# Rounding to integers by casts through int32 instead of a magic constant, in the FFN block of a layer-norm, attention and BitLinear layer on 8 cores

## The chip, the cores and the metric

The kernel runs on the 8 cores of one Trainium2 chip, the same program on each, with no exchange between them. The metric is the device time of the slowest core in microseconds (us). The engines of a core are called PE (TensorE, matrix products and transposes), DVE (VectorE), ACT (ScalarE), POOL (GpSimd) and SP (SyncE, which here only issues DMAs).

## The reference

With `xn = layernorm(x)`, the output is `x + attention(xn) + ffn(xn)`. The change concerns the ffn alone:

```
def act_quant(x):
    scale = 127.0 / jnp.clip(jnp.max(jnp.abs(x), axis=-1, keepdims=True), 1e-05)
    q = jnp.clip(jnp.round(x * scale), -128.0, 127.0) / scale
    return x + jax.lax.stop_gradient(q - x)
def bitlinear158(x, w, b):
    xq = act_quant(rms_norm(x))
    wq = weight_quant(w)
    return jnp.einsum('bsd,od->bso', xq, wq) + b
h = jax.nn.silu(bitlinear158(x, w1, b1))
h = jax.nn.gelu(h, approximate=False)
h = layer_norm(h, ln_g, ln_b)
return bitlinear158(h, w2, b2)
```

x is 4 x 4096 x 2048 float32, w1 is 8192 x 2048, w2 is 2048 x 8192. The two places that matter are the two `jnp.round(x * scale)` on activations: one on the 2048 wide input of w1, one on the 8192 wide input of w2.

## The kernel before

Each core owns 2048 rows (16 tiles of 128) of one of the four batches. The program goes through phases with a barrier of all engines between them: quantising w1 and w2 to ternary values in DRAM (phase_q), layer norm and the K, V and Q projections with rope (phase_a, phase_b1, phase_b2, phase_b3), the ffn (phase_f) and the attention (phase_att), which adds the stored ffn result. The change touches phase_f only.

phase_f works on 8 blocks (index fb) of FB = 256 rows. The activations of a block lie transposed, channel on the partition and row in the free dimension, so one piece is 128 x 256; the hidden layer has OC = 64 such pieces, the model width DC = 16. Every engine has one queue, and the order in it is the order of the code. For block fb, with pb = fb - 1, the queues hold in this order:

- mm1: PE forms 64 products with w1 (L1066, 16 matmuls each, weights fST loaded by SP in 32 loads of 1 MB into two buffers). DVE takes each out of one of four PSUM banks (L1085, L1089), ACT takes a tanh (L1104), DVE multiplies (L1094, a scalar_tensor_tensor), and ACT applies the gelu and the sums for the second layer norm.
- The statistics of that layer norm (small operations on DVE, ACT and PE), and then the loop of DVE that normalises the 64 pieces of fH (L1275 to L1290). Beside it PE forms mm2 of the block before, pb (L850, weights fW in 32 loads of 1 MB into two buffers); after every fourth piece DVE takes one of the 16 results out of PSUM into one of two buffers fTF20 and fTF21 (`evac_mm2`, L863), and ACT adds the bias into fFT (L873).
- `emit_a1(fb + 1)`: the input of the next block. For its two 128 x 2048 tiles DVE and ACT do a layer norm (L431 to L438), then DVE scales and rounds each tile in place (L990 and L993), PE transposes it in 16 pieces (L478) and ACT copies these to fXQT (L493). A scale row is spread over the partitions into bcd (L229).
- The Q2 loop: DVE scales and rounds the 64 pieces of fH to the bf16 integers fQ2, the right operand of mm2. This is the loop of L1372 and L1374. Each piece is two instructions, each with a drain behind it, in which DVE waits until its writes are done:

```
vector.tensor_mul(b["TF"][:, :], H[:, oc * FB:(oc + 1) * FB], s.bcc[:, :])
vector.drain()
ins = vector.tensor_scalar(Q2[:, oc * FB:(oc + 1) * FB], b["TF"][:, :],
                           MAGIC, MAGIC, ALU.add, ALU.subtract)
```

- `emit_b_base(pb)`: PE transposes the 32 pieces of fFT of block pb back through two PSUM banks (L914), DVE adds x (fXN, loaded again from x_own) into fBB (L935), and SP stores fBB to base_scr in four parts. Then mm1 of the next block begins. In block 0 there is no pb, so mm1 of block 1 stands on PE right behind `emit_a1(1)`.

After the eighth block mm2 and the base part of that block follow alone. The rounding uses that adding and subtracting 12582912 (MAGIC) in float32 leaves the nearest integer.

Of the kernel before, what the change touches and what calls it, by code (L numbers as in the profile page):

```python
# [8 lines left out]

F32 = mybir.dt.float32  # L10
BF16 = mybir.dt.bfloat16
AF = mybir.ActivationFunctionType
ALU = mybir.AluOpType
AX = mybir.AxisListType

MAGIC = 12582912.0
NEGBIG = -1.0e9


# [20 lines left out]
class Bld:  # L40
# [745 lines left out]
    def phase_f(self, b):  # L786
        s, c, block = self, self.c, self.block
        D, DC, OC, FB, INNER = c.D, c.DC, c.OC, c.FB, c.INNER
        NT = FB // 128
        H, Q2, XQT = b["H"], b["Q2"], b["XQT"]  # L790

        csx, csd, cq1 = "F_sx", "F_sd", "F_q1"
        ctt, cte2 = "F_ct", "F_ce"
# [10 lines left out]
        cm2, cm2e, cffn = "F_m2", "F_m2e", "F_ff"  # L804
# [7 lines left out]
            s.sem(nm)  # L812
        n_ocg = OC // 4
        OH = OC // 2
        XPO = max(1, D // FB)

        def emit_b_w2(pb, fb2):
# [38 lines left out]

        def evac_mm2(vector, pb, fb2, dc):
            vector.wait_ge(s.sem(cm2), fb2[cm2] + 2 * (dc + 1))
            if dc >= 2:
                vector.wait_ge(s.sem(cffn), fb2[cffn] + dc - 1)  # L860
            elif pb > 0:
                vector.wait_ge(s.sem(cffn), fb2[cffn])
            ins = vector.tensor_mul(b["TF2"][dc % 2][:, :], s.PB[2 + dc % 2][:, 0:FB],  # L863
                                    s.bce[:, :])
            s.inc(ins, cm2e, 1)
# [76 lines left out]

        def emit_a1(fbk):
            t0k = fbk * FB
            a1B = {nm: s.val(nm) for nm in (csd, ctt, "F_Ttp", cq1, csx)}
            XNF, cxn, cfree, base = self.emit_ln(s.x_own[t0k:t0k + FB, :], NT, "F_L", b,
                                                 pre=[(csx, a1B[csx]),
                                                      ("F_Ttp", a1B["F_Ttp"])])
            q1base = a1B[cq1]

            @block.scalar
            def _(scalar):
                for t in range(NT):
                    scalar.wait_ge(s.sem(cxn), base[cxn] + t + 1)
                    ins = scalar.activation(b["SQD"][:, :], XNF[t % 2][:, :], AF.Square,
                                            accum_out=s.fst[:, 16 + t:17 + t])
                    s.inc(ins, csx, 1)
                    scalar.drain()
                    ins = scalar.activation(s.fst[:, 18 + t:19 + t], s.fst[:, 16 + t:17 + t],
                                            AF.Sqrt, bias=s.eps_col[:, 0:1], scale=1.0 / D)  # L960
                    s.inc(ins, csd, 1)

            @block.vector
            def _(vector):
                vector.wait_ge(s.sem(ctt), a1B[ctt])
                for t in range(NT):
                    vector.wait_ge(s.sem(csd), a1B[csd] + t + 1)
                    vector.reciprocal(s.fst[:, 0:1], s.fst[:, 18 + t:19 + t])
                    vector.drain()
                    vector.reduce_max(s.fst[:, 1:2], XNF[t % 2][:, :], AX.X,  # L970
                                      apply_absolute_value=True)
                    vector.drain()
                    vector.tensor_mul(s.fst[:, 2:3], s.fst[:, 0:1], s.fst[:, 1:2])
                    vector.drain()
                    vector.tensor_scalar_max(s.fst[:, 2:3], s.fst[:, 2:3], 1e-5)
                    vector.drain()
                    vector.reciprocal(s.fst[:, 3:4], s.fst[:, 2:3])
                    vector.drain()
                    vector.tensor_mul(s.fst[:, 3:4], s.fst[:, 3:4], s.fst[:, 0:1])
                    vector.drain()  # L980
                    vector.tensor_scalar_mul(s.fst[:, 3:4], s.fst[:, 3:4], 127.0)
                    vector.drain()
                    vector.tensor_mul(s.fst[:, 20 + t:21 + t], s.fst[:, 2:3], s.m1h_sb[:, 0:1])
                    vector.drain()
                    vector.tensor_scalar_mul(s.fst[:, 20 + t:21 + t], s.fst[:, 20 + t:21 + t],
                                             1.0 / 127.0)
                    vector.drain()
                    if t == 0:
                        vector.wait_ge(s.sem("F_Ttp"), a1B["F_Ttp"])
                    vector.tensor_scalar(b["Q1"][t % 2][:, :], XNF[t % 2][:, :],  # L990
                                         s.fst[:, 3:4], MAGIC, ALU.mult, ALU.add)
                    vector.drain()
                    ins = vector.tensor_scalar(b["Q1"][t % 2][:, :], b["Q1"][t % 2][:, :],  # L993
                                               MAGIC, None, ALU.subtract)
                    s.inc(ins, cq1, 1)

            self.emit_transpose(b["Q1"], cq1, None, q1base, NT,
                                lambda t, dc: XQT[:, dc * FB + t * 128: dc * FB + t * 128 + 128],
                                "F_T")

            @block.tensor
            def _(tensor):
                tensor.wait_ge(s.sem(cq1), q1base + NT)
                tensor.wait_ge(s.sem("F_Tte"), s.val("F_Tte"))
                ins = None
                for t in range(NT):
                    ins = tensor.transpose(s.PB[6][0:1, t * 128:t * 128 + 128],
                                           s.fst[:, 20 + t:21 + t], s.ident_f[:, :])
                s.inc(ins, ctt, 1)

            @block.scalar
            def _(scalar):
                scalar.wait_ge(s.sem(ctt), s.val(ctt))
                ins = scalar.copy(s.srow[0:1, 0:FB], s.PB[6][0:1, 0:FB])
                s.inc(ins, cte2, 1)

            self.bcast_row(s.srow[0:1, 0:FB], s.bcd[:, :], FB, 7, "F_cs",
                           cte2, s.val(cte2))

        emit_a1(0)  # L1020
        for fb in range(c.NFB):
# [344 lines left out]
            @block.vector  # L1366
            def _(vector):
                vector.wait_ge(s.sem(f3), s.val(f3))
                if pb >= 0:
                    vector.wait_ge(s.sem(cm2), fB[cm2] + 2 * DC)  # L1370
                for oc in range(OC):
                    vector.tensor_mul(b["TF"][:, :], H[:, oc * FB:(oc + 1) * FB], s.bcc[:, :])  # L1372
                    vector.drain()
                    ins = vector.tensor_scalar(Q2[:, oc * FB:(oc + 1) * FB], b["TF"][:, :],  # L1374
                                               MAGIC, MAGIC, ALU.add, ALU.subtract)
                    s.inc(ins, cq2, 1)
                    vector.drain()

# [466 lines left out]
    def build(self):  # L1845
# [3 lines left out]
        D, KV, DC, OC, FB = c.D, c.KV, c.DC, c.OC, c.FB  # L1849
# [7 lines left out]
        with self.ctx:  # L1857
            for i in range(8):
                self.sem(f"bar{i}")
            with nc.Block() as block:  # L1860
# [3 lines left out]
                if self.upto >= 1:  # L1864
                    st = ExitStack()
                    a = alloc(st, [("qW0", [128, 2048], F32), ("qW1", [128, 2048], F32),
                                   ("qS0", [128, 2048], BF16), ("qS1", [128, 2048], BF16),
                                   ("qT0", [128, 2048], BF16), ("qT1", [128, 2048], BF16)])
# [6 lines left out]
                if self.upto >= 2:  # L1875
# [4 lines left out]
                    a = alloc(st, [("aXA", [128, D], F32), ("aXN0", [128, D], F32),  # L1880
                                   ("aXN1", [128, D], F32), ("aSQ", [128, D], BF16)])
# [5 lines left out]
                    if self.upto >= 3:  # L1887
                        st = ExitStack()
                        a = alloc(st, [("kKH", [128, DC * 512], F32),
                                       ("kWC0", [128, D], BF16), ("kWC1", [128, D], BF16),  # L1890
                                       ("kTR0", [128, 1024], F32), ("kTR1", [128, 1024], F32),
                                       ("kKO0", [128, 512], BF16), ("kKO1", [128, 512], BF16),
                                       ("kRT0", [128, 512], F32), ("kRT1", [128, 512], F32)])
# [6 lines left out]
                    if self.upto >= 4:  # L1900
                        st = ExitStack()
                        a = alloc(st, [("vWV", [128, DC * (D // 2)], BF16),
                                       ("vKO0", [128, 512], BF16), ("vKO1", [128, 512], BF16)])
# [22 lines left out]
                if self.upto >= 6:  # L1926
# [10 lines left out]
                                   ("fHS2", [128, FB], BF16), ("fHS3", [128, FB], BF16),  # L1937
                                   ("fTG0", [128, FB], F32), ("fTG1", [128, FB], F32),
                                   ("fTF", [128, FB], F32),
                                   ("fTF20", [128, FB], F32), ("fTF21", [128, FB], F32),  # L1940
                                   ("fRM", [128, FB], F32),
                                   ("fRN", [128, FB], F32),
                                   ("fW20", [128, (OC // 2) * 128], BF16),
# [7 lines left out]
                                 HB=[a["fHB0"], a["fHB1"], a["fHB2"], a["fHB3"]],  # L1951
                                 HS=[a["fHS0"], a["fHS1"], a["fHS2"], a["fHS3"]],
                                 TG=[a["fTG0"], a["fTG1"]],
                                 TF=a["fTF"], TF2=[a["fTF20"], a["fTF21"]],
                                 XNF0=a["fXN0"], XNF1=a["fXN1"],
                                 RM=a["fRM"], RN=a["fRN"],
                                 W2=[a["fW20"], a["fW21"]], FT=a["fFT"],
# [94 lines left out]
```

## Time and profile before

| | |
|---|---|
| median of 2 runs | 10460.79 us (10424.76 and 10496.82) |
| the profiled execution's own time | 10498.86 us |
| its span on the slowest core (core 4) | 10497.3 us |
| spans of the 8 cores | 10396.2 to 10497.3 us |
| busy on that core | PE 4937.4, DVE 3670.3, ACT 2248.3, POOL 230.3 us |
| phase_f | about 4615 to 8800 us of the span |

The span is the time from the first to the last instruction of a core; the 1.6 us between it and the execution's own time lie around it. No engine is busy for half of the span, so busy shares alone do not say what sets the time: the phases differ, and within phase_f the engines mostly work in turn. The views to read are the waits of an engine (who released it), the instructions in order of time, and the busy time by stretches.

### The profile page before, as it was taken

Reading aid. Unit: us, or ns where it says so; the run is one execution under the profiler, and the core shown is the slowest. Engines: PE = TensorE matmul, PEld = TensorE weight load, DVE = VectorE, ACT = ScalarE, POOL = GpSimd, SP = SyncE. Lnnn points to the kernel's source line nnn. Section 1 sums busy time; section 2 is a strip of 40 time slices with the busy share of each in tenths; the row PEclk is TensorE's granted clock in tenths of the full one; section 3 lists DMA queues with packets and bytes.
Section 4 is the critical chain, followed back from the end, with each engine's and each line's share of the span. In section 5 each row is a group of like instructions: output and inputs, shape, how many; then the busy total and the mean of one; then the engine's idle time right before and its main releaser. Section 6 shows DMA issues by size and latency. Waiting matters only on the chain.

```text
span 10497.3 us, 91973 instructions; the slowest of 8 cores (10396.2 to 10497.3 us)
## 1 busy us (share of the span) xinstructions
PE 4937.4 (47%) x27826; PEld 2905.6 (28%) x28008; DVE 3670.3 (35%) x8144; ACT 2248.3 (21%) x4838; POOL 230.3 (2%) x214
## 2 busy tenths in 40 slices
PE   0000002454456853343566564747484854665656
PEld 0000002221122321222344443435363532222222
DVE  5521113112211012226565747475656541111120
ACT  0055444200001111222313131313141300111110
POOL 0000000011110000000000000000000000000000
PEclk9999995666777876676787777878686877787879
DMA  6678982576772145552344343435352535232324
GB/s 233 245 246 230 177 161 85 91 89 97 95 89 59 48 75 90 87 106 83 121 148 153 133 149 133 169 117 181 115 189 104 188 138 148 89 108 85 116 67 134
DMA packets 949922, 1356.91 MB, mean 129 GB/s; under 512 B 564032, under 2 KB 785600, under 8 KB 840896
## 3 DMA queue, kind: packets, MB, share of 16 engines
q1 hardware_dynamic: 546720, 1233.57, 37.5%
q0 software_dynamic: 402720, 117.45, 11.1%
q8 instruction: 236, 3.87, 0.1%
q14 instruction: 246, 2.02, 0.1%
HBM read 1325.70 MB, written 142.61 MB: 140 GB/s over the span
## 4 chain that ended last, share of the span: by engine, by line
DMA 34%; PE 29%; DVE 20%; ACT 6%; issue 6%; DVEq 4%; SPq 1%; ACTq 0%; POOLq 0%
PE PB L1066 7%; DMA qW<-w2t 5%; PE PB L628 5%; PE PB L746 4%; DMA qW<-w1t 4%; DMA kWC<-wk 4%; DMA fST<-w1q_scr 3%; DMA fW<-w2q_scr 3%; PE PB L850 3%; PE PB L1479 3%; DMA tVB<-v_scr 2%; DVE fTF L1372 2%; DMA q3WC<-wq 2%; DMA kt_scr<-kKO 2%; DMA y<-tOB 2%
## 5 line engine op out<-in xcount | busy, mean ns | idle before, releaser
L850 PE MATMUL PB<-fQ,fW 128*128 128x256 bf16 x8192 | 1000.6, 285 | 252.8 <-DMA fW<-w2q_scr 244.7
L1066 PE MATMUL PB<-fXQT,fST 128*128 128x256 bf16 x8192 | 1022.4, 281 | 200.1 <-DMA fST<-w1q_scr 118.4
L850 PEld LDWEIGHTS PB<-fQ,fW 128*128 128x128 bf16 x8192 | 823.7, 102 | 432.4 <-issue 304.8
L1066 PEld LDWEIGHTS PB<-fXQT,fST 128*128 128x128 bf16 x8192 | 784.6, 100 | 424.6 <-issue 320.2
L628 PE MATMUL PB<-xnT,kWC 128*128 128x512 bf16 x2007 | 606.0, 472 | 606.9 <-ACT kKH L641 338.2
L543 PE MATMUL PB<-ident_f,aXN 128*128 128x128 f32 x512 | 114.2, 416 | 1255.5 <-DVE aXN L530 1003.7
L746 PE MATMUL PB<-vWV,xnT 128*128 128x512 bf16 x2007 | 471.9, 398 | 120.0 <-DMA vWV<-wv 117.2
L628 PEld LDWEIGHTS PB<-xnT,kWC 128*128 128x128 bf16 x2048 | 232.9, 116 | 979.8 <-issue 894.3
L543 PEld LDWEIGHTS PB<-ident_f,aXN 128*128 128x128 f32 x512 | 103.9, 224 | 1265.7 <-issue 1265.7
L399 DVE TENSOR_TENSOR qT<-qS 128x2048 bf16<-128x2048 bf16 x128 | 156.9, 1226 | 806.9 <-ACT qS L387 806.9
L692 DVE TENSOR_TENSOR kRT<-kKH,kTR 128x512 f32<-128x512 f32 x64 | 44.3, 692 | 1001.7 <-ACT kKH L641 789.6
L1690 PE MATMUL PB<-tPT,tVB 128*128 128x512 bf16 x1252 | 313.9, 394 | 165.2 <-DMA tVB<-v_scr 136.5
L1479 PE MATMUL PB<-tKB,tQA 128*128 128x512 bf16 x1128 | 295.2, 426 | 193.8 <-DMA tKB<-kt_scr 192.3
L314 DVE TENSOR_REDUCE absacc<-qW 128x1 f32<-128x2048 f32 x128 | 292.6, 2286 | 260.0 <-DMA qW<-w1t 131.3
L1832 DVE TENSOR_TENSOR tOB<-PB,tBP 128x128 f32<-128x128 f32 x256 | 74.7, 292 | 861.7 <-PE PB L1741 603.3
L914 PE MATMUL PB<-ident_f,fFT 128*128 128x128 f32 x256 | 111.9, 443 | 539.4 <-DVE fBB L935 529.4
L386 ACT ACTIVATE qS<-qW,sm 128x2048 bf16<-128x2048 f32 x128 | 256.2, 2001 | 461.3 <-DMA qW<-w2t 314.8
L628 PE MATMUL PB<-q3XQ,q3WC 128*128 128x512 bf16 x1000 | 280.4, 446 | 135.8 <-DMA q3WC<-wq 128.0
L1094 DVE SCALAR_TENSOR_TENSOR fH<-fTG,fTF 128x256 f32<-128x256 f32 x512 | 217.9, 426 | 354.5 <-ACT fTG L1104 354.5
L1085 DVE TENSOR_TENSOR fTF<-PB,bcd 128x256 f32<-128x256 f32 x512 | 217.6, 425 | 291.8 <-PE PB L1066 283.2
L746 PEld LDWEIGHTS PB<-vWV,xnT 128*128 128x128 bf16 x2048 | 207.8, 102 | 384.1 <-issue 216.3
L641 ACT COPY kKH<-PB 128x512 f32<-128x512 f32 x128 | 74.2, 586 | 1120.1 <-PE PB L628 689.6
(230 smaller groups left out, 6696.5 us busy)
## 6 DMA issues: line engine op xcount, KB each, us to landing
fST<-w1q_scr SPq DMA_DIRECT2D x256, 1024.0 KB, 5.0
fW<-w2q_scr SPq DMA_DIRECT2D x256, 1024.0 KB, 5.2
qW<-w1t SPq DMA_DIRECT2D x128, 1024.0 KB, 6.3
qW<-w2t SPq DMA_DIRECT2D x128, 1024.0 KB, 7.7
tVB<-v_scr SPq DMA_DIRECT2D x160, 512.0 KB, 3.3
kWC<-wk POOLq DMA_DIRECT2D x128, 512.0 KB, 7.4
tKB<-kt_scr SPq DMA_DIRECT2D x40, 1024.0 KB, 7.9
w1q_scr<-qT SPq DMA_DIRECT2D x64, 512.0 KB, 3.5
```

The lines of the kernel that those rows point to most:

```text
L314: ins = vector.reduce_sum(s.absacc[:, na % 64:na % 64 + 1], WROWS[it % 2][:, 0:cw], AX.X, apply_absolute_value=True)
L386: scalar.activation(SGN[0][:, 0:cw], WROWS[it % 2][:, 0:cw], AF.Sign, bias=nmh)
L543: ins = tensor.transpose(bank[:, (dc % 4) * 128:(dc % 4) * 128 + 128], src[:, dc * 128:(dc + 1) * 128], s.ident_f[:, :])
L628: ins = tensor.matmul(bank[:, :], WCB[it % 2][:, dci * 128:(dci + 1) * 128], rhs_cb(tb, dci), start=(dci == 0), stop=(dci == DC - 1))
L746: ins = tensor.matmul(bank[:, 0:VW], s.xnT[:, dci * c.KV + kt * 128: dci * c.KV + kt * 128 + 128], wvh[:, dci * (D // 2) + do * VW: dci * ...
L850: ins = tensor.matmul(bank[:, 0:FB], b["W2"][it % 2][:, oo * 128:(oo + 1) * 128], Q2[:, oc * FB:(oc + 1) * FB], start=(oc == 0), stop=(oc ...
L1066: ins = tensor.matmul(bank[:, 0:FB], b["ST"][g % 2][:, dc * 256 + o2 * 128: dc * 256 + o2 * 128 + 128], XQT[:, dc * FB:(dc + 1) * FB], sta ...
L1085: ins = vector.tensor_mul(b["TF"][:, :], s.PB[MBK[oc % 4]][:, 0:FB], s.bcd[:, :])
L1094: ins = vector.scalar_tensor_tensor(H[:, oc * FB:(oc + 1) * FB], b["TG"][oc % 2][:, :], 1.0, b["TF"][:, :], ALU.add, ALU.mult)
L1372: vector.tensor_mul(b["TF"][:, :], H[:, oc * FB:(oc + 1) * FB], s.bcc[:, :])
L1479: last = tensor.matmul(bank[:, :], b["QA"][:, dc * 512 + il * 128: dc * 512 + il * 128 + 128], b["KB"][nktc % 2][:, d8 * 512:(d8 + 1) * 51 ...
L1690: last = tensor.matmul(s.PB[d8][:, :], b["VB"][nvc % 2][:, dc * 128:(dc + 1) * 128], b["PT"][:, kc * 512:(kc + 1) * 512], start=(kc == 0), ...
```

## The change

Both roundings are done another way. The value is shifted up by 256 (RSH) so that it is positive, cast to int32 (new buffer fQI) and back to float32; a comparison adds one where the fraction is at least a half, and 256 is taken off again. In the Q2 loop a piece is now six instructions in place of two, each followed by a drain. In `emit_a1` the second instruction on a 2048 wide tile is replaced by eight pieces of 256 columns with four instructions each. The two buffers fTF20 and fTF21 become one (fTF20), so `evac_mm2` waits for ACT to have read the previous result (`cffn` one step later than before). Before the first tile of `emit_a1` DVE also waits for the stores of fBB that were issued up to then (F_bs0, F_bs1). The two constants I32 and RSH and a local name DH that is not used are added.

```diff
@@ evac_mm2
-            if dc >= 2:
-                vector.wait_ge(s.sem(cffn), fb2[cffn] + dc - 1)
+            if dc >= 1:
+                vector.wait_ge(s.sem(cffn), fb2[cffn] + dc)
@@ emit_a1
-            a1B = {nm: s.val(nm) for nm in (csd, ctt, "F_Ttp", cq1, csx)}
+            a1B = {nm: s.val(nm) for nm in (csd, ctt, "F_Ttp", cq1, csx,
+                                            "F_bs0", "F_bs1")}
@@
                     if t == 0:
                         vector.wait_ge(s.sem("F_Ttp"), a1B["F_Ttp"])
+                        vector.wait_ge(s.sem("F_bs0"), a1B["F_bs0"])
+                        vector.wait_ge(s.sem("F_bs1"), a1B["F_bs1"])
                     vector.tensor_scalar(b["Q1"][t % 2][:, :], XNF[t % 2][:, :],
-                                         s.fst[:, 3:4], MAGIC, ALU.mult, ALU.add)
-                    vector.drain()
-                    ins = vector.tensor_scalar(b["Q1"][t % 2][:, :], b["Q1"][t % 2][:, :],
-                                               MAGIC, None, ALU.subtract)
+                                         s.fst[:, 3:4], RSH, ALU.mult, ALU.add)
+                    vector.drain()
+                    ins = None
+                    for hq in range(D // FB):
+                        q1c = b["Q1"][t % 2][:, hq * FB:(hq + 1) * FB]
+                        vector.tensor_copy(b["QI"][:, :], q1c)
+                        vector.drain()
+                        vector.tensor_copy(b["TF"][:, :], b["QI"][:, :])
+                        vector.drain()
+                        vector.scalar_tensor_tensor(b["RN"][:, :], q1c, -0.5,
+                                                    b["TF"][:, :], ALU.add, ALU.is_ge)
+                        vector.drain()
+                        ins = vector.scalar_tensor_tensor(q1c, b["TF"][:, :], -256.0,
+                                                          b["RN"][:, :], ALU.add, ALU.add)
+                        vector.drain()
                     s.inc(ins, cq1, 1)
@@ the Q2 loop
                     vector.tensor_mul(b["TF"][:, :], H[:, oc * FB:(oc + 1) * FB], s.bcc[:, :])
                     vector.drain()
-                    ins = vector.tensor_scalar(Q2[:, oc * FB:(oc + 1) * FB], b["TF"][:, :],
-                                               MAGIC, MAGIC, ALU.add, ALU.subtract)
+                    vector.tensor_scalar(b["TF"][:, :], b["TF"][:, :], RSH, None, ALU.add)
+                    vector.drain()
+                    vector.tensor_copy(b["QI"][:, :], b["TF"][:, :])
+                    vector.drain()
+                    vector.tensor_copy(b["RM"][:, :], b["QI"][:, :])
+                    vector.drain()
+                    vector.scalar_tensor_tensor(b["RN"][:, :], b["TF"][:, :], -0.5,
+                                                b["RM"][:, :], ALU.add, ALU.is_ge)
+                    vector.drain()
+                    ins = vector.scalar_tensor_tensor(Q2[:, oc * FB:(oc + 1) * FB],
+                                                      b["RM"][:, :], -256.0,
+                                                      b["RN"][:, :], ALU.add, ALU.add)
                     s.inc(ins, cq2, 1)
                     vector.drain()
@@ buffers
-                                   ("fTF20", [128, FB], F32), ("fTF21", [128, FB], F32),
+                                   ("fQI", [128, FB], I32),
+                                   ("fTF20", [128, FB], F32),
-                                 TF=a["fTF"], TF2=[a["fTF20"], a["fTF21"]],
+                                 TF=a["fTF"], QI=a["fQI"], TF2=[a["fTF20"], a["fTF20"]],
```

The first place is DVE's queue from the last instruction of `emit_a1(1)` into the Q2 loop of block 0. Before (fXN is the input tile, fH the hidden layer, fQ the rounded hidden layer, bcc and bcd scale rows spread over the partitions):

```order
L990 TENSOR_SCALAR fXN<-fXN,fst 128x2048
L993 TENSOR_SCALAR fXN<-fXN 128x2048
L226 UNCONDITIONAL_BRANCH
L229 COPY bcd<-PB 128x256
L1366 UNCONDITIONAL_BRANCH
L1372 TENSOR_TENSOR fTF<-fH,bcc 128x256
L1374 TENSOR_SCALAR fQ<-fTF 128x256
```

The same place on DVE in the changed program, from the last 256 wide piece of `emit_a1(1)` through the first piece of the Q2 loop:

```order
L1002 CAST fQI<-fXN 128x256
L1004 CAST fTF<-fQI 128x256
L1006 SCALAR_TENSOR_TENSOR fRN<-fXN,fTF 128x256
L1009 SCALAR_TENSOR_TENSOR fXN<-fTF,fRN 128x256
L228 UNCONDITIONAL_BRANCH
L231 COPY bcd<-PB 128x256
L1383 UNCONDITIONAL_BRANCH
L1389 TENSOR_TENSOR fTF<-fH,bcc 128x256
L1391 TENSOR_SCALAR fTF<-fTF 128x256
L1393 CAST fQI<-fTF 128x256
L1395 CAST fRM<-fQI 128x256
L1397 SCALAR_TENSOR_TENSOR fRN<-fTF,fRM 128x256
L1400 SCALAR_TENSOR_TENSOR fQ<-fRM,fRN 128x256
```

Nothing has changed places with anything else: the new instructions stand where the old one stood, and the copy of bcd and the loop behind it come after them. The six rows from L1389 to L1400 stand 64 times in a row, and the four from L1002 to L1009 eight times in a row for each tile. DVE has 9804 instructions in the changed program and 7260 before: 4 more for each of 512 pieces and 31 more for each of 16 tiles.

## Rows read from the trace of the kernel before

**Rows 1.** The page: span.

```profile
span 10497.3 us, 91973 instructions; the slowest of 8 cores (10396.2 to 10497.3 us)
```

**Rows 2.** Busy by stretch: length, PE, PEld, DVE, ACT, POOL, PE clock, DMA share, GB/s.

```profile
4615.00:8800.00 4185.00, 2413.21 (x18128) 1785.26 (x18128) 2406.26 (x6280) 1063.55 (x2704) 8.50 (x16) 0.78 0.40 142
```

**Rows 3.** Waits of PE in phase_f: total us, times, longest.

```profile
PE PB L914 <- DVE fBB L935: 529.4, 42, 58.1
PE PB L478 <- DVE fXN L993: 325.3, 16, 91.9
```

**Rows 4.** PE in order of time: around two Q2 loops, start us, us.

```profile
5060.48 8.52 PE L1066 MATMUL PB<-fXQT,fST 128*128 128x256 bf16 x64
5118.96 3.57 PE L1066 MATMUL PB<-fXQT,fST 128*128 128x256 bf16 x16 [49.95 <-DVE fTF L1085]
...
5575.74 3.88 PE L914 MATMUL PB<-ident_f,fFT 128*128 128x128 f32 x8 [58.10 <-DVE fBB L935]
...
5613.83 6.38 PE L1066 MATMUL PB<-fXQT,fST 128*128 128x256 bf16 x31 [7.54 <-DMA fST<-w1q_scr]
```

**Rows 5.** DVE in order of time: the Q2 loop of block 0.

```profile
5061.00 0.41 DVE L1372 TENSOR_TENSOR fTF<-fH,bcc 128x256 f32<-128x256 f32 x1
5061.49 0.29 DVE L1374 TENSOR_SCALAR fQ<-fTF 128x256 bf16<-128x256 f32 x1
5061.88 0.43 DVE L1372 TENSOR_TENSOR fTF<-fH,bcc 128x256 f32<-128x256 f32 x1
...
5117.86 0.29 DVE L1374 TENSOR_SCALAR fQ<-fTF 128x256 bf16<-128x256 f32 x1
5118.38 0.42 DVE L1085 TENSOR_TENSOR fTF<-PB,bcd 128x256 f32<-128x256 f32 x1 [0.23 <-issue]
```

**Rows 6.** Groups of DVE by line and shape: busy us, mean ns, idle before.

```profile
L1372 DVE TENSOR_TENSOR fTF<-fH,bcc 128x256 f32<-128x256 f32 x512 | 218.0, 426 | 49.0 <-issue 3.2
L1094 DVE SCALAR_TENSOR_TENSOR fH<-fTG,fTF 128x256 f32<-128x256 f32 x512 | 217.9, 426 | 354.5 <-ACT fTG L1104 354.5
L1374 DVE TENSOR_SCALAR fQ<-fTF 128x256 bf16<-128x256 f32 x512 | 150.4, 294 | 41.6 <-issue 2.6
L1285 DVE COPY fRM<-fH 128x256 f32<-128x256 f32 x8 | 2.4, 294 | 0.7
L229 DVE COPY bcc<-PB 128x256 f32<-128x256 f32 x8 | 3.4, 425 | 36.7 <-PE PB L222 36.7
L692 DVE TENSOR_TENSOR kRT<-kKH,kTR 128x512 f32<-128x512 f32 x64 | 44.3, 692 | 1001.7 <-ACT kKH L641 789.6 <-DMA kt_scr<-kKO 212.1
```

**Rows 7.** DVE in order of time: rounding the two tiles in emit_a1(2).

```profile
5499.23 1.29 DVE L990 TENSOR_SCALAR fXN<-fXN,fst 128x2048 f32<-128x2048 f32 x1
5500.60 1.23 DVE L993 TENSOR_SCALAR fXN<-fXN 128x2048 f32<-128x2048 f32 x1
5501.74 0.16 DVE L968 RECIPROCAL fst<-fst 128x1 f32<-128x1 f32 x1
```

**Rows 8.** PE in order of time: the transposes of the second tile.

```profile
5508.71 3.65 PE L478 MATMUL PB<-ident_f,fXN 128*128 128x128 f32 x16 [3.09 <-DVE fXN L993]
```

**Rows 9.** Busy by stretch: mm1, mm2, the Q2 loop of block 1; columns as rows 2.

```profile
5120.00:5275.00 155.00, 135.45 (x1088) 96.30 (x1086) 77.47 (x198) 94.00 (x260) 0.00 (x0) 0.96 0.58 204
5290.00:5440.00 150.00, 114.18 (x900) 93.01 (x900) 119.91 (x296) 8.76 (x16) 0.00 (x0) 0.90 0.51 190
...
5516.00:5574.90 58.90, 1.64 (x4) 0.58 (x4) 46.36 (x129) 0.00 (x0) 0.00 (x0) 0.50 0.01 4
```

**Rows 10.** The costliest groups of the page: the matmuls of mm2 and mm1.

```profile
L850 PE MATMUL PB<-fQ,fW 128*128 128x256 bf16 x8192 | 1000.6, 285 | 252.8 <-DMA fW<-w2q_scr 244.7
L1066 PE MATMUL PB<-fXQT,fST 128*128 128x256 bf16 x8192 | 1022.4, 281 | 200.1 <-DMA fST<-w1q_scr 118.4
```

**Rows 11.** DVE and ACT in order of time: a result of the last mm2.

```profile
8608.52 0.43 DVE L863 TENSOR_TENSOR fTF<-PB,bce 128x256 f32<-128x256 f32 x1 [9.37 <-PE PB L850]
...
8609.04 0.51 ACT L873 ACTIVATE fFT<-fTF,b2r_sb 128x256 f32<-128x256 f32 x1 [9.29 <-DVE fTF L863]
```

More of the change, by code:

```diff
@@ L10 @@
 F32 = mybir.dt.float32
+I32 = mybir.dt.int32
 BF16 = mybir.dt.bfloat16
@@ L16 @@
 MAGIC = 12582912.0
+RSH = 256.0
 NEGBIG = -1.0e9
@@ L814, in phase_f @@
         OH = OC // 2
+        DH = D // 2
         XPO = max(1, D // FB)
```

## The prediction

> **What bounds the kernel now.** I went from the whole to the place. The page gives a span of 10497.3 us [rows 1], and the busy time by stretches says that phase_f takes 4185 us of it, with PE busy for 2413 and DVE for 2406 of these [rows 2]. Two engines that are each busy for 58% of a stretch and idle for the rest are either both waiting for a third or for each other. So the next view is who waited for whom: in phase_f PE sat for 529.4 us in front of the transposes of the ffn result (L914) until DVE had done an addition, 42 times and once for 58.1 us, and for 325.3 us in front of the transposes of the rounded input (L478) until DVE had rounded it, 16 times [rows 3]. The engines take turns, and in these two places it is DVE's turn.
>
> The order of time shows what DVE does then. Around the Q2 loop of block 1 the next transposes wait for 58.10 us, and around that of block 0 the next products of mm1 wait for 49.95 us, after the 64 matmuls that fit into the four free banks took 8.52 us [rows 4]. In block 0 the loop runs from 5061.00 us to 5118.38 us, which is when the first use of a mm1 result (L1085) starts: 64 pieces in 57.4 us, 0.89 us each, with no wait for another engine between them [rows 5]. In the stretch of block 1's loop PE is busy for 1.64 us, ACT for none and the DMA engines at a share of 0.01 [rows 9]. So the Q2 loop stands alone on the path to the end in each of the 8 blocks, and what is added to it is added to the time. Behind it the 32 additions start, their four stores and the second load of x follow in series, and the loads of mm1 are issued only after that (7.54 us of waiting for fST before mm1 [rows 4]). None of these lies beside the loop, so a longer loop hides none of them.
>
> The rounding in `emit_a1` is in series too. The first tile's L993 ends and the second tile's work follows on DVE at once [rows 7]; the transposes of the second tile wait for the second L993 (3.09 us idle, releaser L993) [rows 8], and the copies, the row bcd and the Q2 loop hang on these.
>
> **The change part by part.** Prices first. At 128x256 a tensor_scalar with constants takes 294 ns, a copy in SBUF 294, a two-operand instruction 426, and a scalar_tensor_tensor on two float32 operands also 426 [rows 6]. Between two instructions with a drain between them about 0.08 us pass: L1372 and L1374 take 426 + 294 = 720 ns and repeat every 0.89 us [rows 5, 6], so 0.17 for two.
>
> Q2 loop, for each piece. Unchanged: the multiplication. Removed: one tensor_scalar of 0.294. Added: one tensor_scalar (0.294 + 0.08 = 0.374), two casts, two scalar_tensor_tensor. For a cast between float32 and int32 there is no row. It is a copy with one source, both sides in SBUF, four bytes in and four out. The nearest row is the copy from SBUF to SBUF, 294 ns; the other end is the copy out of PSUM, 425 ns, which is also what a two-operand instruction takes. L1374 also changes the type (float32 to bf16) and is at 294. I take 0.294 + 0.08 = 0.374 a cast. No row of this width with one or two operands is under 286 to 294 ns, so I see no end below. The scalar_tensor_tensor with the comparison: 0.426 + 0.08 = 0.506. The last one takes the place of the removed instruction: 0.426 - 0.294 = 0.132. Sum: 0.374 + 2 x 0.374 + 0.506 + 0.132 = 1.76 us. With 64 pieces and 8 blocks: 512 x 1.76 = 901 us. A piece then takes 2.65 us and a loop 170 us.
>
> The Trainium skill bears on the cast: VectorE: DVE Perf Modes, section "What auto-detection actually checks", says that an instruction with one source takes two elements a cycle when source and destination are in SBUF, whatever the type. By that rule the casts cost what the SBUF copy does, and the sum stays; without it they cost what the copy from PSUM does.
>
> `emit_a1`, for each tile. Removed: L993, 1.14 us from its start to the next instruction on the first tile and 1.23 us to its end on the second [rows 7], so 1.2. Added: eight times two casts and two scalar_tensor_tensor, each with a drain: 8 x (2 x 0.374 + 2 x 0.506) = 14.1 us. Net 12.9 us, and with 16 tiles 206 us. The first tile's transposes now run beside the second tile's rounding as before; the second tile's wait grows from 3.09 us to about 16.
>
> One buffer for fTF2: in the last mm2 DVE's evacuation starts at 8608.52 us, ACT reads the buffer from 8609.04 for 0.51 us, and DVE had idled 9.37 us before its turn [rows 11]. The new wait is over some 8 us before it matters: nothing. Were the cover gone, it would be 1.03 us for each of 15 results in 8 blocks, 124 us. The waits for the fBB stores name stores issued a block earlier, which were over before DVE came to this point: nothing; without that cover, at most a wait like the 7.54 us for a DMA in rows 4, 8 times, 60 us.
>
> Sum: 901 + 206 = 1107 us. The profiled execution took 10498.86 us, so it would be 11606. Its own time lies 38 us above the median of the runs shown (10460.79 us), and I forecast the median: 11568 us, about 10.6% more.
>
> **The rivals.**
>
> The casts run at one element a cycle. For: no row has int32 in it. Against: a changed type does not slow L1374, and the copies. There are 2 x (512 + 128) = 1280 casts, each 425 - 294 = 131 ns longer: +168 us, 11736 us. The full sum would then be 1275 us.
>
> PE's clock gives something back. The granted clock is 0.96 in mm1, 0.90 in mm2 and 0.50 in the Q2 loop [rows 9]. If longer rests of the array led to the full clock in all of mm1 and mm2, 16384 matmuls of 256 columns would take 107 ns at 2.4 GHz, 1748 us in place of 1000.6 + 1022.4 = 2023 [rows 10]: at most 275 us back, so 11293 us. Against: the array already rests for 58 us in each block and these stretches are near the full level, and mm2 waits for its weights for 244.7 us beside [rows 10], so a faster clock there would largely turn into waiting. The opposite, later starts at the half level, is as small: transposes and mm1's first products behind the loop start at 0.50 already.
>
> The comparison is dear. In the scalar_tensor_tensor, two float32 operands in SBUF might stream at half the rate: 256 columns more, which by the step from 426 ns at 256 columns to 692 at 512 [rows 6] is 266 ns. 1280 such instructions give +340 us, 11908 us. Against it stands L1094, the same instruction on two float32 operands in SBUF, at 426 ns in 512 cases [rows 6]. The Trainium skill, Vector Engine (DVE) Microarchitecture Reference, section "7. Points that are easy to get wrong", says that this instruction form with two SBUF sources other than bf16 has half the throughput; that is this rival if it is read against one element a cycle, and the trace does not agree with that reading.
>
> Not slower. For that the added time must lie under something else that ends later anyway: one mechanism, DVE's two stretches not being what the next stage waits for. The most that lies beside a Q2 loop is mm1's first 8.52 us in block 0 [rows 4], already covered now, and 1.64 us of PE in block 1 [rows 9]. To stay within 2% (209 us) some 900 of the 1107 us would have to be covered, 112 us in each block; fully covered it would be 10461 us. The rows speak against it in every block. That the change does not do what it says could only mean that a drain costs nothing, or that instructions overlap: without the 0.08 us gaps the sum would be about 1107 - (4 x 512 + 32 x 16) x 0.08 = 902 us, 11363 us; the gaps are seen in rows 5, with the same drains.
>
> **How the numbers follow.** The forecast with casts as copies: 0.80. Casts at the lower rate: 0.11. Clock giving back over 60 us, or gaps smaller than counted: 0.05. The dear comparison: 0.03. Not slower: 0.01. Within the forecast's own case, the two runs of before differ by 72 us, and gap and cover add some 40 us either way: 11490 to 11650. The range must reach over the second case, which holds most of the rest: 11460 to 11760 us. A measurement of this kernel can tell about 2% from no change. Faster by over 2%: 0.005. Within 2%: 0.015. Slower: 0.98.
>
> **What would show it.** Right: the casts at 294 ns and the scalar_tensor_tensor at 426; a piece of the Q2 loop every 2.65 us and the loop 170 us; PE's longest wait before L914's transposes near 171 us; 15.5 us in place of 2.6 for rounding a tile; mm1 and mm2 stretches as long as before; the phases outside phase_f unchanged. Wrong: casts near 425 ns (rival one); a scalar_tensor_tensor near 690; an idle DVE inside the Q2 loop or before an evacuation of mm2 that ACT releases (the wait on one buffer); or a Q2 loop whose growth PE or DMA work fills.

## The result, and the profile after

The changed kernel takes 11528.42 us (median of 11 runs, 11456.07 to 11604.1); the kernel before took 10420.11 us beside it (10 runs). The ratio is 1.104, with a 95% interval of 1.1003 to 1.1076: 1108 us more. The forecast was 11568 us, from a sum of 1107 us. Every ratio here is formed from fast executions alone (the cores of one chip half sometimes run some per cent slower together), so it can differ by up to 0.6% from the quotient of the medians given beside it.

Line numbers in the rows of a changed kernel or of an experiment are those of that kernel's own code.

The groups of DVE of the changed kernel, in the columns of [rows 6]:

```profile
L1400 DVE SCALAR_TENSOR_TENSOR fQ<-fRM,fRN 128x256 bf16<-128x256 f32 x512 | 217.9, 426 | 38.5
...
L1397 DVE SCALAR_TENSOR_TENSOR fRN<-fTF,fRM 128x256 f32<-128x256 f32 x512 | 217.5, 425 | 40.4 <-issue 3.1
...
L1391 DVE TENSOR_SCALAR fTF<-fTF 128x256 f32<-128x256 f32 x512 | 150.5, 294 | 39.6 <-issue 0.6
L1393 DVE CAST fQI<-fTF 128x256 int32<-128x256 f32 x512 | 150.5, 294 | 39.7 <-issue 3.1
L1395 DVE CAST fRM<-fQI 128x256 f32<-128x256 int32 x512 | 150.5, 294 | 38.8 <-issue 1.7
```

The casts, for which the trace before had no row, cost 294 ns in both directions, what the copy and the tensor_scalar cost in [rows 6]. The comparison (L1397) costs what the other scalar_tensor_tensor does. The last column gives the idle time ahead of all 512, 0.08 us for each instruction.

DVE in order of time, the first and the last piece of the Q2 loop of block 0, against [rows 5]:

```profile
5011.94 0.41 DVE L1389 TENSOR_TENSOR fTF<-fH,bcc 128x256 f32<-128x256 f32 x1
5012.44 0.29 DVE L1391 TENSOR_SCALAR fTF<-fTF 128x256 f32<-128x256 f32 x1
5012.80 0.29 DVE L1393 CAST fQI<-fTF 128x256 int32<-128x256 f32 x1
5013.17 0.29 DVE L1395 CAST fRM<-fQI 128x256 f32<-128x256 int32 x1
5013.54 0.43 DVE L1397 SCALAR_TENSOR_TENSOR fRN<-fTF,fRM 128x256 f32<-128x256 f32 x1
5014.04 0.43 DVE L1400 SCALAR_TENSOR_TENSOR fQ<-fRM,fRN 128x256 bf16<-128x256 f32 x1
5014.56 0.42 DVE L1389 TENSOR_TENSOR fTF<-fH,bcc 128x256 f32<-128x256 f32 x1
...
5180.12 0.43 DVE L1400 SCALAR_TENSOR_TENSOR fQ<-fRM,fRN 128x256 bf16<-128x256 f32 x1
5180.78 0.42 DVE L1102 TENSOR_TENSOR fTF<-PB,bcd 128x256 f32<-128x256 f32 x1 [0.23 <-issue]
```

From one multiplication to the next a piece takes 2.62 us, and the loop takes 168.8 us, against 0.89 and 57.4 before: 111.4 us more, and 8 x 111.4 = 891 us.

PE around it, which answers to [rows 4] and [rows 8]:

```profile
4983.85 3.65 PE L480 MATMUL PB<-ident_f,fXN 128*128 128x128 f32 x16 [42.39 <-DVE fXN L1009]
5003.40 3.64 PE L480 MATMUL PB<-ident_f,fXN 128*128 128x128 f32 x16 [15.91 <-DVE fXN L1009]
...
5011.43 9.93 PE L1083 MATMUL PB<-fXQT,fST 128*128 128x256 bf16 x64
5181.35 3.38 PE L1083 MATMUL PB<-fXQT,fST 128*128 128x256 bf16 x16 [159.99 <-DVE fTF L1102]
```

PE waits 159.99 us where it waited 49.95. Its wait for the second tile is 15.91 us where it was 3.09 in block 1 [rows 8] and in block 0. Its wait for the first tile is 42.39 us, where the trace before has at the same place:

```profile
5046.13 3.65 PE L478 MATMUL PB<-ident_f,fXN 128*128 128x128 f32 x16 [29.60 <-DVE fXN L993]
5052.87 3.48 PE L478 MATMUL PB<-ident_f,fXN 128*128 128x128 f32 x16 [3.09 <-DVE fXN L993]
```

Each is 12.8 us longer, and 16 x 12.8 = 205 us. The waits of PE in phase_f, against [rows 3]:

```profile
PE PB L917 <- DVE fBB L938: 1296.9, 42, 170.4
```

Again 42 times, and the longest went from 58.1 to 170.4 us. A stretch of mm1, one of mm2 and the Q2 loop of block 0, in the columns of [rows 9] (the lengths are those asked for, not those of the stages):

```profile
5180.00:5335.00 155.00, 137.78 (x1084) 97.55 (x1084) 77.23 (x194) 91.18 (x252) 0.00 (x0) 0.95 0.57 204
5355.00:5510.00 155.00, 120.58 (x1005) 99.86 (x1006) 126.13 (x313) 10.25 (x17) 0.00 (x0) 0.94 0.59 208
5012.00:5180.00 168.00, 9.36 (x63) 7.15 (x60) 137.54 (x384) 0.00 (x0) 0.00 (x0) 0.52 0.03 13
```

Such windows catch different parts of a stage, so the stages were also measured whole, over all blocks and cores. From DVE's first evacuation of mm1 to its first normalising instruction a block takes 178 to 186 us before and 178 to 183 after. The normalising, beside which mm2 runs, takes 158 to 159 us in both from block 1 on. The mean granted clock went from 0.909 to 0.923 in the first of these stages and from 0.892 to 0.895 in the second: the longer rests of PE gave nothing back that can be seen. The clock is 0.52 in the window of the Q2 loop, close to the lower level of 0.50, so the longer loop adds time near that level, and the mean over the whole program fell on all cores (0.789 to 0.798 before, 0.772 to 0.778 after).

**A ruler inside the trace.** Whole times scatter by one per cent, and the trace shows one place: DVE's first evacuation of mm1 came 4591 to 4685 us after the start on the eight cores of one and the same execution before. So I also measure each kernel by the stretch from DVE's first evacuation of mm1 to its last of mm2, on each core, and take the median of the eight. On the profile's slowest core of before and of after its ends are the first and last starts in these rows:

```profile
L1085 DVE TENSOR_TENSOR fTF<-PB,bcd x512: 424/425/427, 4669.2 to 8274.8; 128x256 f32<-128x256 f32 x171
L863 DVE TENSOR_TENSOR fTF<-PB,bce x128: 424/425/426, 5303.9 to 8742.6; 128x256 f32<-128x256 f32 x128
```

```profile
L1102 DVE TENSOR_TENSOR fTF<-PB,bcd x512: 423/425/427, 4598.5 to 9144.7; 128x256 f32<-128x256 f32 x171
L866 DVE TENSOR_TENSOR fTF<-PB,bce x128: 424/425/427, 5371.3 to 9706.0; 128x256 f32<-128x256 f32 x128
```

| kernel | stretch, median of 8 cores (range), us | against before |
|---|---|---|
| before | 4037 (4017 to 4073) | |
| changed | 5087 (5078 to 5108) | +1050 |
| changed, on the later chip (e8) | 5100 (5084 to 5115) | +1063 |
| e1: Q2 loop alone | 4909 (4902 to 4930) | +872 |
| e2: emit_a1 alone | 4197 (4183 to 4210) | +159 |
| e3: one fTF2 buffer alone | 4040 (4017 to 4077) | +3 |
| e4: 512 columns wide | 4754 (4719 to 4784) | +717 |
| e5: cast does the rounding | 4017 (4007 to 4027) | -20 |
| e6: ACT casts | 3747 (3732 to 3780) | -290 |
| e7: half the drains | 4838 (4832 to 4885) | +801 |

The stretch holds all 8 Q2 loops and 14 of the 16 tiles; the two tiles of block 0 lie ahead of it and should bring 2 x 12.8 = 26 us more, too little to be seen there. Inside it the working above would give 891 + 14 x 12.8 = 1070 us; 1050 and 1063 were measured.

What varies inside the stretch from trace to trace is mostly mm1. The eight mm1 of a core took together (median of the cores) 1434 to 1442 us in the traces of the changed kernel, e1, e2 and e5, where the granted clock in them was 0.92, and 1453 to 1463 us in those of before, e3, e4 and e7, where it was 0.89 to 0.91; e6 and e8 lie between. The change does not set this: e5 has loops as short as before and is the shortest. The 14 tiles gave 181 us between before and changed, as worked out; mm1 came out 13 us shorter.

### The profile page after: what moved, and what is told of

Read it like the earlier page. It is cut to its first block, busy times and chain, and to the rows that moved or that the text cites. A ratio compares the mean times of both kernels' runs of the same rounds, so it can differ in the third digit from the quotient of the medians.

```text
span 11468.8 us, 97276 instructions; the slowest of 8 cores (11386.0 to 11468.8 us)
## 1 busy us (share of the span) xinstructions
PE 4879.4 (43%) x28008; PEld 2878.7 (25%) x28008; DVE 4571.7 (40%) x10688; ACT 2247.7 (20%) x4838; POOL 230.7 (2%) x214
## 4 chain that ended last, share of the span: by engine, by line
DMA 30%; DVE 26%; PE 26%; issue 6%; ACT 6%; DVEq 4%; SPq 1%; another core or an unknown queue 0%; ACTq 0%; POOLq 0%
PE PB L1083 6%; PE PB L630 5%; DMA qW<-w2t 5%; PE PB L748 4%; DMA fST<-w1q_scr 3%; DMA qW<-w1t 3%; DMA kWC<-wk 3%; DMA fW<-w2q_scr 3%; PE PB L1506 3%; PE PB L853 2%; DMA tVB<-v_scr 2%; DVE fQ L1400 2%; DVE fRN L1397 2%; DVE fTF L1389 2%; DMA q3WC<-wq 2%
## 5 line engine op out<-in xcount | busy, mean ns | idle before, releaser
L748 PE MATMUL PB<-vWV,xnT 128*128 128x512 bf16 x2048 | 447.0, 382 | 116.1 <-DMA vWV<-wv 116.1
L917 PEld LDWEIGHTS PB<-ident_f,fFT 128*128 128x128 f32 x256 | 45.8, 182 | 1375.2 <-issue 1375.2
```

The costliest lines, as they stand in the source:

```text
L748: ins = tensor.matmul(bank[:, 0:VW], s.xnT[:, dci * c.KV + kt * 128: dci * c.KV + kt * 128 + 128], wvh[:, dci * (D // 2) + do * VW: dci * ...
```

## The experiments

All ratios are to the kernel before on the same chip.

**Which part costs what: e1 and e2.** e1 is the changed kernel with the old rounding in `emit_a1`:

```diff
-                                         s.fst[:, 3:4], RSH, ALU.mult, ALU.add)
-                    vector.drain()
-                    ins = None
-                    for hq in range(D // FB):
...
+                                         s.fst[:, 3:4], MAGIC, ALU.mult, ALU.add)
+                    vector.drain()
+                    ins = vector.tensor_scalar(b["Q1"][t % 2][:, :], b["Q1"][t % 2][:, :],
+                                               MAGIC, None, ALU.subtract)
```

> The changed kernel with the rounding in emit_a1 put back to the magic constant; the new Q2 loop and the single fTF2 buffer stay. Theory (the Q2 loop stands alone on the path): 512 pieces, each about 1.74 us longer, so +891 us, ratio to before about 1.086. Rival (the two stretches share some cover, or the 1.104 of the whole is made by the single buffer too): the ratio is under 1.075, or over 1.095.

Measured: ratio 1.0756, interval 1.069 to 1.0822 (4 runs, median 11317.11 us, against 10503.12). The stretch is 872 us longer than before.

e2 is the changed kernel with the old two instructions a piece in the Q2 loop.

> The changed kernel with the Q2 loop put back to two instructions a piece; the new rounding in emit_a1 and the single fTF2 buffer stay. Theory: 16 tiles, each 12.8 us longer, all of it in series, +205 us, ratio about 1.020. Rival (PE's transposes and ACT's copies of the first tile hide the longer rounding of the second): half or less, ratio 1.010 or under. Together with e1 the sum must be the 1.104 of the whole if the parts are independent.

Measured: ratio 1.0102, interval 1.0008 to 1.0195 (4 runs, median 10675.99 us). The stretch is 159 us longer.

By whole times neither run decides. Both forecasts (1.086 and 1.020) lie just outside the measured intervals, the bounds of the rivals (1.075 and 1.010) lie inside, and the two ratios add up to 1.086 and not to 1.104. By the ratios the runs lack some 100 us each, by the medians 77 us and 32 us. The stretch decides: it grew by 872 of 891 us and by 159 of 179, together 1031 us, against 1050 for the whole change. The rival of e2, a cover of half or more, would be 90 us or less. In e2 the stages that hold the 14 tiles grew by 180 us and mm1 was 18 us shorter; in e1 mm1 was 11 us shorter. So the parts are independent and nothing of either is hidden.

The traced executions themselves lack little. On the same chip e3, whose one edit costs nothing as shown below, has a longest span of 10482.4 us; that of e1 is 11370.2, 888 us more, and that of e2 10657.5, 175 us more. e1's three other executions were shorter by 15 to 105 us than the traced one; where they were shorter, no trace shows, so that stays open.

**The single buffer: e3.** The kernel before, with this alone:

```diff
-            if dc >= 2:
-                vector.wait_ge(s.sem(cffn), fb2[cffn] + dc - 1)
+            if dc >= 1:
+                vector.wait_ge(s.sem(cffn), fb2[cffn] + dc)
...
-TF2=[a["fTF20"], a["fTF21"]]
+TF2=[a["fTF20"], a["fTF20"]]
```

> The kernel before with the single fTF2 buffer and its wait alone. Theory: the wait is over some 8 us before it matters, ratio 1.000, and no idle time of DVE before L863 that ACT releases. Rival: evacuations of mm2 are held up by ACT, up to 1.03 us each, 124 us in all, ratio up to 1.012.

Measured: ratio 1.0006, interval 0.9969 to 1.0043 (12 runs); the rival's 1.012 is out. What DVE waited for ahead of the evacuation:

```profile
DVE fTF L863 <- PE PB L850: 163.6, 35, 15.7
...
DVE fTF L863 <- issue: 20.3, 93, 0.6
```

ACT is not among the releasers. The second buffer bought nothing in this kernel.

**The fixed part of an instruction: e4.** The changed kernel with twice the width, the scratch in fXA, which is free in both places. In the Q2 loop:

```diff
+                for op in range(OC // 2):
+                    for u in range(2):
...
+                    vector.tensor_scalar(WT, WT, RSH, None, ALU.add)
+                    vector.drain()
+                    vector.tensor_copy(WI, WT)
+                    vector.drain()
+                    vector.tensor_copy(WF, WI)
+                    vector.drain()
+                    vector.scalar_tensor_tensor(WR, WT, -0.5, WF, ALU.add, ALU.is_ge)
...
```

> The changed kernel with the added instructions 512 columns wide instead of 256 (in both places; only the multiplication by bcc stays at 256), with the input buffer fXA as scratch. Theory (about half of each added instruction is a fixed part: 294 ns at 256 columns against 427 at 512 for one operand, 426 against 692 for two, and one gap in place of two): a pair of pieces takes 4.04 us in place of 5.28, a tile 10.2 in place of 14.0, in all 379 us less than the changed kernel, ratio to before about 1.068. Rival (the time goes by columns, fixed parts overlap): no gain, ratio 1.104.

Measured: ratio 1.0637, interval 1.0582 to 1.0693. The rival is out. The prices at 512 columns:

```profile
L1408 DVE SCALAR_TENSOR_TENSOR fXA<-fXA 128x512 f32<-128x512 f32 x256 | 177.2, 692 | 19.6 <-issue 0.4
L1404 DVE CAST fXA<-fXA 128x512 int32<-128x512 f32 x256 | 109.4, 427 | 19.3 <-issue 0.4
```

```profile
PE PB L917 <- DVE fBB L938: 1029.8, 42, 131.8
```

294 ns for 256 columns and 427 for 512 mean 0.52 ns a column and 161 ns that every instruction pays; with the gap of 0.08 us, two thirds of a narrow cast is fixed cost. For two operands, 426 and 692 ns mean 1.04 ns a column and 160 ns, so that about half is fixed. The wait beside a Q2 loop fell from 170.4 to 131.8 us, 38.6 for the 39.7 that 32 x 1.24 promised. The stretch is 333 us shorter than that of the changed kernel, where 8 x 38.6 + 14 x 3.8 = 362 were due; the eight mm1 took 23 us more in this trace, at a granted clock of 0.90 in place of 0.92.

**Is int32 the price: e5.** The changed kernel with the cast doing the rounding:

```diff
+                    vector.tensor_mul(b["QI"][:, :], H[:, oc * FB:(oc + 1) * FB], s.bcc[:, :])
+                    vector.drain()
+                    ins = vector.tensor_copy(Q2[:, oc * FB:(oc + 1) * FB], b["QI"][:, :])
```

and in `emit_a1` one 2048 wide multiplication written as int32 and one 2048 wide cast back.

> The cast to int32 does the rounding itself, so nothing is shifted or compared: two instructions a piece in the Q2 loop (multiplication written as int32, cast to bf16) and two 2048 wide ones a tile in emit_a1. Theory (the price is the number of instructions and their width, int32 costs nothing): loops of 57 us as before, phase_f stretch near the 4037 us of before, ratio 1.000. Rival (int32 as the output of a two-operand instruction, or a cast 2048 wide, is slow): the multiplication over 426 ns or the cast over 294, each 0.13 us more a piece, 68 us, ratio 1.007 or more.

Measured: ratio 1.0038, interval 1.0 to 1.0076; stretch 4017 us.

```profile
L1378 DVE TENSOR_TENSOR fQI<-fH,bcc 128x256 int32<-128x256 f32 x512 | 217.4, 425 | 49.5 <-issue 4.8
L1380 DVE CAST fQ<-fQI 128x256 bf16<-128x256 int32 x512 | 150.5, 294 | 37.6
```

The interval alone does not exclude the rival's 1.007, but the prices do: 425 and 294 ns are those of before. A loop with two instructions a piece and int32 in it takes the time of before. So the 10% are four more instructions a piece and 31 more a tile, not the type.

**The drains: e7.** The changed kernel with two pieces side by side in the Q2 loop:

```diff
...
+                    for u in range(2):
+                        vector.tensor_copy(SL[2 + u].bitcast(I32), SL[u])
+                    vector.drain()
+                    for u in range(2):
+                        vector.tensor_copy(SL[4 + u], SL[2 + u].bitcast(I32))
+                    vector.drain()
...
```

> The changed kernel with two pieces interleaved in the Q2 loop (scratch in fXA), each step for both pieces and one drain behind the two, so half the drains and the same instructions. Theory (an instruction without a drain ahead overlaps the one before: 0.34 us from L1288 to L1290 and 0.21 from L1285 to L1286 in the trace of before, against 0.50 and 0.37 with one): a pair takes 4.26 us in place of 5.24, 250 us less than the changed kernel, ratio to before about 1.079. Rival (the Trainium skill, VectorE: DVE Perf Modes, section The DRAIN you can't avoid: the engine empties after each instruction whether or not a drain stands there): no gain, ratio 1.104.

Measured: ratio 1.0793, interval 1.0711 to 1.0875; stretch 249 us shorter than that of the first trace of the changed kernel, 262 than that of e8. DVE in order of time, two instructions to a row:

```profile
5139.31 0.75 DVE L1392 TENSOR_TENSOR fXA<-fH,bcc 128x256 f32<-128x256 f32 x2
5140.14 0.49 DVE L1396 TENSOR_SCALAR fXA<-fXA 128x256 f32<-128x256 f32 x2
5140.71 0.50 DVE L1399 CAST fXA<-fXA 128x256 int32<-128x256 f32 x2
...
5142.68 0.76 DVE L1409 SCALAR_TENSOR_TENSOR fQ<-fXA 128x256 bf16<-128x256 f32 x2
5143.53 0.76 DVE L1392 TENSOR_TENSOR fXA<-fH,bcc 128x256 f32<-128x256 f32 x2
```

Two of 426 ns take 0.76 us together, less than their sum; a pair of pieces takes 4.22 us (5.24 before). So independent instructions overlap where no drain stands between them. The Trainium skill, VectorE: DVE Perf Modes, section "The DRAIN you can't avoid", says that "the next op does not start until the 8-stage pipe empties", and also that "A next op that is not held starts earlier", where held, by the same page, means made to wait until every earlier instruction of the engine has finished. The recorded rival took the first sentence without the second, and so read it does not hold here. Whether groups of more than two pieces would save more was not tried.

**A faster kernel: e6.** The kernel before, with the Q2 loop split between two engines:

```diff
+                    if oc >= 8:
+                        vector.wait_ge(s.sem(cq2), q20 + oc - 7)
+                    ins = vector.tensor_mul(QS[oc % 8], H[:, oc * FB:(oc + 1) * FB],
+                                            s.bcc[:, :])
+                    s.inc(ins, "F_qm", 1)
...
+                    scalar.wait_ge(s.sem("F_qm"), s.val("F_qm") - OC + oc + 1)
+                    ins = scalar.copy(Q2[:, oc * FB:(oc + 1) * FB], QS[oc % 8])
+                    s.inc(ins, cq2, 1)
```

> The kernel before, but in the Q2 loop DVE multiplies into int32 without drains (eight slots in fXA) and ACT, idle there before, casts to bf16. emit_a1 and the two fTF2 buffers as before. Theory (the Q2 loop alone is on the path): the slower of DVE (0.34 us a piece where L1288 and L1290 follow without a drain) and ACT (0.31 to 0.45 us a piece) sets it, 22 to 30 us a loop in place of 57, so 220 to 280 us less, ratio 0.973 to 0.979. Rival (something else ends just behind the loop, the loads of x or mm1): under 100 us less, ratio over 0.990.

Measured: ratio 0.9698, interval 0.9631 to 0.9765 (10169.6 us against 10466.09); the stretch is 290 us shorter than before. It beats both kernels. The first Q2 loop, by groups:

```profile
L1379 DVE TENSOR_TENSOR fXA<-fH,bcc 128x256 int32<-128x256 f32 x64 | 21.5, 415 | 0.0
L1390 ACT CAST fQ<-fXA 128x256 bf16<-128x256 int32 x64 | 20.3, 402 | 0.0
```

```profile
PE PB L917 <- DVE fBB L938: 257.8, 42, 22.2
```

64 multiplications take 21.5 us without drains, ACT keeps up behind them, and PE's longest wait fell from 58.1 to 22.2 us: 35.9 a block, 287 us in 8. That the whole of it arrives in the time is the same statement as the prediction's, from the other side: nothing stands close behind the Q2 loop. How much of it is due to the second engine and how much to the missing drains was not tried apart.

**The measure again: e8**, the changed kernel unaltered.

> The changed kernel once more on the chip of these runs, as the measure for e4 and e7. Theory: ratio to before 1.10, phase_f stretch 5087 us as in its first trace. Rival (the first ratio held chance from the phases ahead of phase_f, whose length differed by up to 94 us among the cores of one run): ratio under 1.095, with the same phase_f stretch.

Measured: ratio 1.1002, interval 1.0907 to 1.1096; stretch 5100 us. The interval of these 4 runs does not exclude the rival's 1.095 by itself, but the ratio and the stretch both came again: the first ratio was not chance. (e4 ran on another chip, so e8 is the measure for e7 and not for e4.)

## Why the prediction was right

- **The Q2 loop and the rounding of `emit_a1` are alone on the path.** Right. PE's waits grew by what DVE's loop grew (170.4 - 58.1 = 112.3 us against 111.4), e1 and e2 add up, and e6 gives back all that it saves.
- **Prices.** A cast was put at 0.374 us with its gap, a scalar_tensor_tensor at 0.506; the trace has 0.37 and 0.50. A piece was forecast at 2.65 us (2.62 measured), a loop at 170 (168.8), the added time of a tile at 12.9 (12.8). None of the terms of the sum was off by more than one or two per cent.
- **The unknown price**, the cast, was taken from the copy in SBUF and not from the one out of PSUM. That was right. The rule of the Trainium skill (VectorE: DVE Perf Modes, "What auto-detection actually checks") agrees with the trace of e4: a cast takes 0.52 ns a column, and an instruction with two sources 1.04, twice as much.
- **The single buffer and the fBB waits at nothing.** Right for the buffer (e3). The waits for the stores stand ahead of L996 in the changed kernel; the trace shows 2.3 us of idle time there in all, 8 times 0.3 us, put to "issue" and not to a DMA, where L990 before had none. They were not tried alone.
- **The rivals.** Casts at one element a cycle: out, 294 ns. The dear comparison: out, 425 ns. The clock giving back: out as an effect of the longer loops; over all blocks the granted clock was 0.923 in mm1 and 0.895 in mm2 (0.909 and 0.892 before), e5 has the same 0.923 in mm1 with the short loops, and the stretch lacks at most 20 us of the working. Not slower: out.
- **The sum.** 1107 us forecast, 1108 us between the medians. That they agree to one us is luck: the stretch and the two first tiles give 1050 + 26 = 1076 us in the first trace and 1063 + 26 = 1089 in the second, and whole times scatter by more than the rest. The two profiled executions are only 971 us apart, because the part of the span outside the stretch took 6424 us before and 6361 after on their slowest cores. The time itself was put 40 us too high, because the two runs of before that were shown had a median 41 us over that of ten.
- **The chances.** "Not slower" has 0.01 among the cases and 0.02 in the last line (0.005 and 0.015); the two do not agree, and the result does not depend on it.

## What to carry to other kernels

Find the stretches in which one engine works and the others wait; there each added instruction counts in full, and its cost is the fixed part (here 161 ns and a gap of 0.08 us) plus columns, so at 256 columns about half to two thirds of an instruction is paid for its being there, and the count of instructions matters as much as what they compute. Before such a stretch is made longer, look who idles beside it: moving one of two instructions to the idle ACT and leaving out drains between independent pieces took 3% off the whole kernel. Where whole times scatter, measure an edit by a stretch inside the trace that begins and ends in its own phase.

## What was not expected of the hardware

- DVE's independent instructions of 426 ns follow each other every 0.34 us without a drain (21.5 us for 64 in e6), and of 294 ns every 0.2 us (0.49 us for two in e7).
- ACT reads int32 and writes bf16 at 402 ns for 256 columns, and it kept up with DVE at 0.34 us a piece with a semaphore wait in front of each.
- A two-operand instruction on DVE writes int32 at the price of float32 (425 ns).
- The cores of one execution before reach DVE's first evacuation of mm1 up to 94 us apart, and 136 in e2 (4576 to 4712 us), with the same program and without exchange. The causes were not looked into.
